# A four-layer graph network on one core: edge preparation moved into two earlier phases, and norm and dense product made one phase

## The chip, the core and the metric

One NeuronCore of a Trainium2 chip runs the whole program. Its engines work side by side and meet by semaphores: TensorE (PE in the rows; PEld is its loading of stationary operands), VectorE (DVE), ScalarE (ACT), GpSimd (POOL) and SyncE (SP), and 16 DMA engines that move data. The metric is the device time of one execution in microseconds. The kernel before took 6511.56 us, the median of three runs (6511.35 to 6515.23).

## What is computed

The graph has N = 3125 nodes with D = 128 features and E = 100000 edges, sorted by destination. Four layers follow each other, and each ends in `x = layernorm(x + layer(x))`:

```python
x = _layernorm(x + L0(x))   # two transformer convolutions, 8 heads
x = _layernorm(x + L1(x))   # [x, mean of x over the edges] @ W.T + b
x = _layernorm(x + L2(x))   # GINE: three message layers over the edges
x = _layernorm(x + L3(x))   # attention by source, one layer
# L2, one message layer:
m   = relu(h[src] + edge_attr @ W_ee + b_ee) * edge_weight
agg = segment_sum(m, dst)
h   = relu(mlp((1 + eps) * h + agg))
# _layernorm: (x - mean) / sqrt(var + 1e-5) over the 128 features
```

The change lies around L1 and L2. L1 is a dense product of x and a mean aggregation; L2 begins with the dense product h = x W_enc + b_enc and then needs, for each edge, its source row, its 16 attributes, its weight, and whether it has the same destination as its neighbour.

## The kernel before

Nodes are held as 25 tiles of 128 partitions x 128 features, side by side in one tile `x` (128 x 3200 floats); `skip` and `work` are of the same shape. `big` is one large scratch area cut into named parts. `QUADS` are the tiles in groups of four: six of four tiles and one of one.

The program is a row of phases, each an `nc.Block()`: every engine gets its own list of instructions, and at the block's end all engines meet. Semaphores got by `fresh` are cleared on POOL behind the block. `Chain` (`link(...)`) makes VectorE wait for the end of each instruction before it begins the next.

From the second convolution to the first message layer the phases are, in this order:

1. `node_math(conv_nodes)` (L1445 to L1457 with `norm_ops`, L988 to L1000): the sums of the heads are divided (L1450), the skip path and x are added (L1451, L1455), and the norm follows: reduce (L992), subtract (L994), square (L995), reduce (L996), square root on ScalarE (recorded as L1024), scale (L1000). Each is one VectorE instruction over 128 x 3200.
2. `node_linear` (L1031 to L1093): SP loads weights (L1042), PE transposes x (L1064), ScalarE copies the turned tiles (L1056), PE multiplies (L1079), VectorE adds the bias (L1092).
3. `by_src(x, False)` (L1468 to L1522), the mean aggregation: 30 indirect loads of 128 x 3200 counts from `snap_tab` by POOL (L1481) into a ring of nine buffers; VectorE takes the difference of two of them (L1505, 25 times), PE multiplies x with it into seven PSUM banks (L1520, 14 passes each). POOL's load v waits for PE's product v - 9.
4. `node_math(per_degree)` (L1560 to L1562): one over the degree.
5. `turn_back` (L1529 to L1551): the sums leave PSUM (L1536, L1548) and are multiplied back node by node (L1564, L1565).
6. `node_math(add_norm)` (L1567 to L1569): add x, then the norm as in 1.
7. `node_linear` again, for h = x W_enc + b_enc.
8. `gine_prep` (L1123 to L1217): VectorE clears the tiles (L1172 to L1177), then SP loads destinations, sources and weights of all edges (L1142), small weights (L1143 to L1146) and all attributes (L1148, 6.4 MB), and writes the table of h that the edges gather from (L1151). VectorE computes which neighbours share a destination (L1184 to L1217), with small products on PE between (L1159 to L1167). SP waits for all of it at the end (L1152 to L1154).
9. `gine_edges`, `gine_nodes`, three times. In `gine_edges` POOL gathers 8 rows per edge unit from `h_tab` (L1241, 784 per layer), PE multiplies attributes (L1281), VectorE joins, weights and scans, ScalarE writes the sums out.

After the third message layer, `node_math(add_norm)` and `node_linear` come once more, for L3, then `by_src(skip, True)` with attention.

Of the kernel before, what the change touches and what calls it, by code (L numbers as in the profile page):

```python
# [40 lines left out]
U = 5  # L41
# [39 lines left out]
def build(nc, a, out):  # L81
    ctx = ExitStack()
    with ctx:
# [904 lines left out]
        def norm_ops(link, act_sqrt, src3, dst3):  # L988

            mean, var, inv, tmp = (col25[:, k * NT:(k + 1) * NT] for k in range(4))  # L990
            bc = lambda c: c.unsqueeze(2).to_broadcast([P, NT, D])
            link(nc.vector.tensor_reduce(mean, src3, AX_X, ALU.add))  # L992
            link(nc.vector.tensor_scalar(mean, mean, 1.0 / D, None, ALU.mult))
            link(nc.vector.tensor_tensor(dst3, src3, bc(mean), ALU.subtract))  # L994
            link(nc.vector.tensor_tensor(sq3, dst3, dst3, ALU.mult))  # L995
            link(nc.vector.tensor_reduce(var, sq3, AX_X, ALU.add))  # L996
            link(nc.vector.tensor_scalar(var, var, 1.0 / D, LN_EPS, ALU.mult, ALU.add))
            act_sqrt(var, tmp)
            link(nc.vector.reciprocal(inv, tmp))
            link(nc.vector.tensor_tensor(dst3, dst3, bc(inv), ALU.mult))  # L1000

# [25 lines left out]
        SQRT = (ACT.Sqrt, col25[:, NT:2 * NT], col25[:, 3 * NT:4 * NT], {})  # L1027

        QUADS = [(t, min(t + 4, NT)) for t in range(0, NT, 4)]

        def node_linear(source, loads, cols, parts, tabs):  # L1031

            with ExitStack() as ph:
                w_in, tr_done, copied, mm_done, evac, tab_out = fresh(ph, "w_in", "tr_done", "copied", "mm_done", "evac", "tab_out")
                turned = [stages[:, k * 512:(k + 1) * 512] for k in range(2)]
                wide = cols > D
                evacs_of = (lambda t: t * len(parts)) if wide else (lambda t: -(-t // 4))
                with nc.Block() as block:
                    @block.sync
                    def _(sp):  # L1040
# [3 lines left out]
                        for lo, hi in QUADS if tabs else ():  # L1044
                            sp.wait_ge(evac, evacs_of(hi))
# [13 lines left out]
                    def _(pe):  # L1059
# [9 lines left out]
                        for g, (lo, hi) in enumerate(QUADS):  # L1069
# [3 lines left out]
                            if not wide:  # L1073
                                later(pe, evac, g - 5)
                            for t in range(lo, hi):
                                if wide:
                                    later(pe, evac, evacs_of(t - 5))
                                to = bank[2 + t % 6][:, 0:cols] if wide else bank[2 + g % 6][:, (t - lo) * D:(t - lo + 1) * D]
                                nc.tensor.matmul(to, turned[g % 2][:, (t - lo) * P:(t - lo + 1) * P], wgt[:, 0:cols], start=True, stop=True).then_inc(mm_done, 1)  # L1079

                    @block.vector
                    def _(dve):
                        dve.wait_ge(w_in, 16 * len(loads))
                        for g, (lo, hi) in enumerate(QUADS):
                            if wide:
# [37 lines left out]
        def gine_prep():  # L1123

            with ExitStack() as ph:
# [6 lines left out]
                with nc.Block() as block:  # L1132
# [5 lines left out]
                    def _(sp):  # L1138
                        sp.wait_ge(cleared, 6)
                        for tile, flat in ((dst_nat, a["dst"]), (src_nat, a["src"]), (weight_nat, a["edge_weight"])):  # L1140
                            for to, of in natural_parts(tile, flat, 1):
                                sp.dma_start(to, of).then_inc(idx_in, 16)  # L1142
# [548 lines left out]
```

## Time and profile before

| | us |
|---|---|
| median of 3 runs | 6511.56 |
| the profiled execution | 6520.61 |
| its span, first to last instruction | 6518.6 |
| VectorE busy in the span | 4148.0 (64%) |
| GpSimd busy in the span | 4155.0 (64%) |
| TensorE busy in the span | 3342.7 (51%) |
| mean granted TensorE clock | 0.673 |

The profile names each instruction by engine, line and the tiles that it writes and reads. "idle before" is the time its engine stood still ahead of it, with what it waited for; `<-issue` is time without a wait that the profile shows, `PEq` and `DVEq` are sequencers at a phase's meeting point. The granted clock is a share of TensorE's 2.4 GHz: 0.50 is its lower level of 1.2 GHz. "SPq" rows are the issue of a DMA, not its transfer.

### The profile page before, as it was taken

What the parts mean: (1) busy time and instruction counts of PE and PEld (TensorE: products, weight loads), DVE (VectorE), ACT (ScalarE), POOL (GpSimd) and SP (SyncE); (2) the same over time, 40 slices, a digit from 0 to 9 for tenths busy, and PEclk for the clock granted to TensorE, in tenths of its full rate; (3) what the DMA queues carried; (4) which work ended last, traced back from release to release, by engine and by line L of the source; (5) the groups of instructions that cost most, each with busy time, mean ns of one, the idle gap of its engine ahead of it and who ended that gap; (6) DMA issues with size and microseconds to landing.
All of it is one profiled execution on the core that took longest, in us unless ns stands there. A gap on an engine that the chain in (4) does not pass through costs nothing. (4 is left out here: it accounts for less than half of the span.)

```text
span 6518.6 us, 51793 instructions
## 1 busy us (share of the span) xinstructions
PE 3342.7 (51%) x13823; PEld 2045.6 (31%) x13823; DVE 4148.0 (64%) x5215; ACT 1487.1 (23%) x3019; POOL 4155.0 (64%) x4233
## 2 busy tenths in 40 slices
PE   3577777746777776553333333433334333433363
PEld 2355555635556555331111111111111111111131
DVE  5577777776777777564555554555554555555597
ACT  0122222201222221002322232222322223222121
POOL 0477777736777775216777776777776777777220
PEclk7677777776776777776556666555556666665686
DMA  0566666627666664543333332333332333333341
GB/s 22 156 198 198 197 195 194 193 82 205 192 194 197 195 198 132 200 148 101 104 107 104 104 104 86 107 104 104 107 105 89 101 104 106 106 104 102 123 158 60
DMA packets 540777, 877.86 MB, mean 135 GB/s; under 512 B 85157, under 2 KB 383121, under 8 KB 532318
## 3 DMA queue, kind: packets, MB, share of 16 engines
q0 software_dynamic: 167776, 479.21, 25.6%
q1 hardware_dynamic: 372728, 395.35, 18.8%
q8 instruction: 130, 2.13, 0.1%
q14 instruction: 143, 1.17, 0.1%
HBM read 553.75 MB, written 320.47 MB: 134 GB/s over the span
## 5 line engine op out<-in xcount | busy, mean ns | idle before, releaser
L1241 POOL DMA_INDIRECT big<-h_tab,big x2352 | 2224.4, 946 | 801.7 <-issue 801.7
L1281 PE MATMUL psum<-big 128*128 128x512 f32 x1176 | 1085.0, 1077 | 1787.4 <-ACT big L1264 1787.2
L633 POOL DMA_INDIRECT big<-kv_tab,big x1664 | 1649.5, 991 | 534.8 <-issue 499.6
L1307 DVE TENSOR_TENSOR psum<-psum,big 128x1024 f32<-128x1024 f32 x294 | 555.5, 1890 | 1363.5 <-DMA big<-h_tab,big 1363.5
L1281 PEld LDWEIGHTS psum<-big 128*128 128x128 f32 x1176 | 342.7, 322 | 2364.4 <-ACT big L1264 2060.9
L1258 ACT COPY big<-big 128x1024 f32<-128x1024 f32 x294 | 563.3, 1916 | 2103.5 <-DVE big L1301 2103.5
L762 PE MATMUL psum<-big 128*128 128x136 f32 x3328 | 715.2, 368 | 480.0 <-DVE big L820 302.2
L762 PEld LDWEIGHTS psum<-big 128*128 128x128 f32 x3328 | 613.9, 259 | 576.1 <-issue 548.4
L672 ACT COPY big<-psum 125x128 f32<-125x128 f32 x1408 | 376.5, 267 | 1488.8 <-PE psum L718 1409.4
L1301 DVE TENSOR_TENSOR_SCAN big<-big,psum 128x1024 f32<-128x1024 bf16 x294 | 669.0, 2276 | 0.1
L710 PE MATMUL psum<-big 128*128 x4992 | 585.6, 265 | 104.5 <-DVE big L791 104.2
L718 PE MATMUL psum<-big 128*128 128x128 bf16 x1408 | 567.5, 403 | 113.5 <-ACT big L672 60.0
L807 DVE TENSOR_TENSOR big<-psum,big 128x512 f32<-128x512 f32 x416 | 286.5, 689 | 418.3 <-DMA big<-kv_tab,big 376.9
L710 PEld LDWEIGHTS psum<-big 128*128 128x128 bf16 x4992 | 447.4, 117 | 194.9 <-issue 111.3
L1481 POOL DMA_INDIRECT big<-snap_tab,small x60 | 138.5, 2309 | 408.3 <-PE psum L1520 266.2
L1313 DVE SCALAR_TENSOR_TENSOR psum<-psum,big 128x1024 f32<-128x1024 f32 x294 | 359.4, 1223 | 0.4
L843 DVE SCALAR_TENSOR_TENSOR big<-big,psum 128x136 f32<-128x136 f32 x832 | 292.2, 351 | 50.8 <-PE psum L762 6.1
L1266 ACT CAST big<-big 128x1024 bf16<-128x1024 f32 x294 | 304.2, 1035 | 0.0
L820 DVE TENSOR_TENSOR big<-big,small 128x512 f32<-128x512 f32 x416 | 286.4, 688 | 0.0
L812 DVE TENSOR_TENSOR big<-big 128x512 f32<-128x512 f32 x416 | 284.9, 685 | 0.2
L817 DVE TENSOR_REDUCE big<-big 128x32 f32<-128x512 f32 x416 | 282.1, 678 | 0.7
L718 PEld LDWEIGHTS psum<-big 128*128 128x128 bf16 x1408 | 209.8, 149 | 219.9 <-issue 171.5
(385 smaller groups left out, 3242.6 us busy)
## 6 DMA issues: line engine op xcount, KB each, us to landing
run_tab<-big SPq DMA_DIRECT2D x294, 512.0 KB, 2.7
snap_tab<-big SPq DMA_DIRECT2D x176, 448.0 KB
item_tab<-big SPq DMA_DIRECT2D x208, 272.0 KB, 4.2
big<-loc_tab SPq DMA_DIRECT2D x104, 512.0 KB, 4.7
big<-h_tab,big POOLq DMA_INDIRECT x2352, 2.5
big<-kv_tab,big POOLq DMA_INDIRECT x1664
snap_tab<-big SPq DMA_DIRECT2D x176, 52.0 KB
kv_tab<-big SPq DMA_DIRECT2D x12, 512.0 KB, 2.6
```

The costliest lines, as they stand in the source:

```text
L633: nc.gpsimd.indirect_dma_start(out=kv[:, b % SLOTS, k, :], out_offset=None, in_=kv_tab, in_offset=bass.IndirectOffsetOnAxis(ap=src_item[:, ...
L672: nc.scalar.copy(snaps[0:125, n % 16 * P:(n % 16 + 1) * P], bank[7][0:125, 0:P]).then_inc(snapped, 1)
L710: ins_ = nc.tensor.matmul(bank[b % 2][:, k * P:(k + 1) * P], hot_T[b // 4 % 2][:, (b % 4 * 4 + k) * P:(b % 4 * 4 + k + 1) * P], q3[:, j * ...
L718: nc.tensor.matmul(bank[7][:, 0:P], key_hot[n // 8 % 2][:, n % 8::8], lo_hot[n // 8 % 2][:, n % 8::8], start=first_c + n == 0, stop=True, ...
L762: ins_ = nc.tensor.matmul(region(2 * b + i), hot[b % 2][:, k * P:(k + 1) * P], va[b % 2][:, k, :], start=s == 0, stop=s == 1)
L1241: nc.gpsimd.indirect_dma_start(out=got[j % RING][:, k * D:(k + 1) * D], out_offset=None, in_=h_tab, in_offset=bass.IndirectOffsetOnAxis(ap ...
L1258: nc.scalar.copy(rows_out[j % ROWS].rearrange("p (t f) -> p f t", f=D), sums_ft[j % DEEP].rearrange("p (f t) -> p f t", t=UNIT)).then_inc( ...
L1266: nc.scalar.copy(inner_x[j % DEEP].rearrange("p (f t) -> p f t", t=UNIT), inner[:, UNIT * j:UNIT * (j + 1)].unsqueeze(1).to_broadcast([P, ...
L1281: ins_ = nc.tensor.matmul(bank[2 * (j % DEEP) + k][:, :], ea_T[j % DEEP], w_blocks[:, k * 512:(k + 1) * 512], start=True, stop=True)
L1301: nc.vector.tensor_tensor_scan(sums_ft[j % DEEP], inner_x[j % DEEP], msg[j % DEEP], 0.0, ALU.mult, ALU.add).then_inc(run_done, 1)
L1307: nc.vector.tensor_tensor(by_feature(msg[j % DEEP]), by_feature(msg[j % DEEP]), got[j % RING].rearrange("p (t f) -> p f t", f=D), ALU.add) ...
L1313: nc.vector.scalar_tensor_tensor(by_feature(msg[j % DEEP]), by_feature(msg[j % DEEP]), 0.0, weight_nat[:, UNIT * j:UNIT * (j + 1)].unsquee ...
```

## The change

- `norm_ops` is gone. A new phase `norm_linear` does the join with x, the norm and the dense product in one block, quad by quad: VectorE joins and takes the mean, ScalarE squares (one instruction per tile, with the sum taken on the way) and takes the root, VectorE scales, PE transposes, ScalarE copies, PE multiplies, VectorE adds the bias. It takes the place of phases 1's norm and 2, of 6 and 7, and of the same pair ahead of L3. For L2 it also writes `h_tab`.
- `gine_prep` is gone. Its memsets, index, weight and small loads, and its chain on VectorE and PE are spread over `by_src(x, False)`, behind the steps n = 4, 8, 12, 14, 18 and 20; `per_degree` is the last of them.
- The edge attributes load in `turn_back`, issued by SP and not waited for there; POOL clears their last rows and makes the node numbers.
- What needs the edge counts (eight short instructions) stands at the head of the first `gine_edges`.
- Areas in `big` and the divisor `den` are placed anew; `gine_edges`, `gine_nodes` and the first convolution are otherwise the same.

```diff
+        def norm_linear(loads, joined, work3, scale_of=None, h_table=False):
...
+                    @block.scalar
+                    def _(act):
+                        for n in range(last + 1):
+                            if n < last:
+                                lo, hi = QUADS[n]
+                                act.wait_ge(centre, n + 1)
                                 for t in range(lo, hi):
+                                    nc.scalar.activation(x3[:, t, :], work3[:, t, :], ACT.Square, bias=mean[:, t:t + 1], accum_out=var[:, t:t + 1]).then_inc(squared, 1)
+                            if n > 0:
+                                lo, hi = QUADS[n - 1]
+                                act.wait_ge(varied, n)
+                                nc.scalar.activation(root[:, lo:hi], var[:, lo:hi], ACT.Sqrt).then_inc(rooted, 1)
+                                act.wait_ge(tr_done, n)
+                                later(act, mm_done, n - 2)
+                                nc.scalar.copy(turned[(n - 1) % 2][:, 0:(hi - lo) * D], bank[(n - 1) % 2][:, 0:(hi - lo) * D]).then_inc(copied, 1)
+                    @block.tensor
+                    def _(pe):
+                        for g, (lo, hi) in enumerate(QUADS):
+                            pe.wait_ge(normed, hi)
+                            later(pe, copied, g - 1)
...
+                            if g == 0:
+                                pe.wait_ge(w_in, 16 * len(loads))
+                            pe.wait_ge(copied, g + 1)
...
+                        def centred(g):
+                            lo, hi = QUADS[g]
+                            joined(link, lo, hi, work3)
+                            link(nc.vector.tensor_reduce(mean[:, lo:hi], work3[:, lo:hi, :], AX_X, ALU.add))
+                            nc.vector.tensor_scalar(mean[:, lo:hi], mean[:, lo:hi], -1.0 / D, None, ALU.mult).then_inc(centre, 1)
...
+                        def scaled(g):
+                            lo, hi = QUADS[g]
+                            dve.wait_ge(rooted, g + 1)
+                            link(nc.vector.reciprocal(inv[:, lo:hi], root[:, lo:hi]))
+                            for t in range(lo, hi):
+                                nc.vector.tensor_scalar(x3[:, t, :], work3[:, t, :], mean[:, t:t + 1], inv[:, t:t + 1], ALU.add, ALU.mult).then_inc(normed, 1)
...
+                        for n in range(last + 3):
+                            if n < last:
+                                centred(n)
+                            if 0 < n <= last:
+                                spread_of(n - 1)
+                            if n >= 3:
+                                product_out(n - 3)
+                            if 0 < n <= last:
+                                scaled(n - 1)
...
+                    @block.sync
+                    def _(sp):
+                        if not attention:
+                            sp.wait_ge(cleared, 5)
+                            for tile, flat_ in ((dst_nat, a["dst"]), (src_nat, a["src"]), (weight_nat, a["edge_weight"])):
+                                for to, of in natural_parts(tile, flat_, 1):
+                                    sp.dma_start(to, of).then_inc(idx_in, 16)
...
+                        between = {} if attention else {4: compared, 8: linked, 12: runs, 14: spread_out, 18: rows_back, 20: degrees}
...
+                            if n in between:
+                                between[n]()
...
+                            if n == 12:
+                                pe.wait_ge(to_pe, 3)
...
+        def turn_back(per_tile, after, attributes=False):
...
+                        if attributes:
+                            (to0, of0), (to1, of1), (to2, of2) = natural_parts(ea_nat, a["edge_attr"].rearrange("e c -> (e c)"), EA)
+                            sp.dma_start(to0[0:96], of0[0:96]).then_inc(ea_in, 16)
+                            sp.wait_ge(cleared, 1)
+                            sp.dma_start(to0[96:112], of0[96:112]).then_inc(ea_in, 16)
+                            sp.dma_start(to1, of1).then_inc(ea_in, 16)
+                            sp.dma_start(to2, of2).then_inc(ea_in, 16)
...
+                        if layer == 0:
+                            pe.wait_ge(totalled, 1)
+                            nc.tensor.matmul(bank[5][:, 0:1], upper[:, :], in_all[:, 0:1], start=True, stop=True).then_inc(in_all_done, 1)
+                            pe.wait_ge(ea_in, 16 * 4)
                         turn(0)
...
-        gine_prep()
+        norm_linear([(wgt[:, 0:D], a["L2_W_enc"]), (bias[:, 0:D], a["L2_b_enc"].to_broadcast([P, D])),
+                                (bn[:, :], a["L2_bn"]), (epsb[:, 0:3], a["L2_eps"].to_broadcast([P, 3]))], plus_x,
+                    area(6400, NT * D).rearrange("p (t d) -> p t d", d=D), h_table=True)
```

## Rows read from the trace of the kernel before

**Rows 1.** Stages: length, busy us of PE, PEld, DVE, ACT, POOL, clock, DMA share, GB/s.
```profile
2623.90:2669.40 45.50, 10.56 (x75) 10.00 (x75) 34.59 (x20) 5.23 (x9) 0.00 (x0) 0.59 0.02 5
2669.40:2697.10 27.70, 0.00 (x0) 0.00 (x0) 0.00 (x1) 0.00 (x0) 8.47 (x9) 0.55 0.90 374
...
2760.00:2800.00 40.00, 40.00 (x105) 18.66 (x104) 25.63 (x17) 0.00 (x0) 16.70 (x8) 1.00 0.81 304
...
2838.30:2854.80 16.50, 12.18 (x50) 11.99 (x50) 9.39 (x30) 1.73 (x4) 0.00 (x0) 0.90 0.00 0
2855.10:2877.50 22.40, 0.00 (x0) 0.00 (x0) 21.61 (x9) 0.22 (x1) 0.00 (x0) 0.54 0.00 0
2877.50:2893.60 16.10, 11.60 (x75) 11.04 (x75) 4.35 (x7) 3.79 (x7) 0.00 (x0) 0.69 0.05 10
2893.60:2911.50 17.90, 0.00 (x0) 0.00 (x0) 7.96 (x6) 0.00 (x0) 2.91 (x1) 0.61 0.27 74
2911.50:2931.90 20.40, 3.04 (x12) 2.78 (x12) 17.46 (x32) 0.00 (x0) 0.00 (x0) 0.50 1.02 249
2931.90:2949.00 17.10, 0.00 (x0) 0.00 (x0) 0.00 (x0) 0.00 (x0) 0.00 (x0) 0.50 0.77 174
...
6081.60:6103.90 22.30, 0.00 (x0) 0.00 (x0) 21.61 (x9) 0.22 (x1) 0.00 (x0) 0.52 0.00 0
6103.90:6122.50 18.60, 11.75 (x75) 11.19 (x75) 4.35 (x7) 3.79 (x7) 0.00 (x0) 0.66 0.10 22
```
**Rows 2.** The longest waits from 2690 to 2840 us: waiter, releaser, total, times, longest.
```profile
DVE big L1505 <- DMA big<-snap_tab,small: 73.5, 25, 27.8
...
PE psum L1520 <- DVE big L1505: 32.0, 1, 32.0
```
**Rows 3.** Timeline: start, length, engine, line, count, idle before; the aggregation.
```profile
2700.71 4.64 PE L1520 MATMUL psum<-big,x 128*128 128x512 f32 x5 [32.01 <-DVE big L1505]
...
2819.53 18.65 PE L1520 MATMUL psum<-big,x 128*128 128x512 f32 x49
...
2826.87 3.49 DVE L1505 SCALAR_TENSOR_TENSOR big<-big 128x3200 f32<-128x3200 f32 x1 [2.47 <-DMA big<-snap_tab,small]
```
**Rows 4.** Timeline of the preparation's loads and of the gathers behind it.
```profile
2911.56 1.09 SPq L1148 DMA_DIRECT2D big<-in_edge_attr  x3
...
2950.50 0.98 POOL L1241 DMA_INDIRECT big<-h_tab,big  x1 [53.31 <-issue]
```
**Rows 5.** What SP's queue waited for, 2600 to 3000 us.
```profile
SPq L1154 <- DMA big<-in_edge_attr: 28.1, 1, 28.1
```
**Rows 6.** DMA issues, 2902 to 2955 us: count, KB each, median us to landing.
```profile
h_tab<-big SPq DMA_DIRECT2D x5, 320.0 KB, 30.6
```
**Rows 7.** Groups of instructions by form: busy us, mean ns, idle before.
```profile
L1056 ACT COPY big<-psum 128x512 f32<-128x512 f32 x30 | 17.6, 587 | 163.9 <-PE psum L1064 163.9
...
L1024 ACT ACT_TABLE_LOAD x4 | 5.1, 1283 | 45.1 <-PEq L872 38.5 <-PEq L1531 6.5
...
L1403 ACT ACTIVATE skip<-skip 128x128 f32<-128x128 f32 x3 | 0.9, 296 | 0.0
```
**Rows 8.** Timeline: VectorE's form with a scalar per partition, four in a row.
```profile
2616.41 0.87 DVE L931 TENSOR_SCALAR big<-big 128x128 f32<-128x128 f32 x4
```
**Rows 9.** Groups by line, whole span: the 512-column VectorE form, and the gathers.
```profile
L1241 POOL DMA_INDIRECT big<-h_tab,big x2352 | 2224.4, 946 | 801.7 <-issue 801.7
...
L812 DVE TENSOR_TENSOR big<-big 128x512 f32<-128x512 f32 x416 | 284.9, 685 | 0.2
```
**Rows 10.** Timeline from a last table row of h to the next gather.
```profile
3990.18 0.29 DVE L1386 SCALAR_TENSOR_TENSOR big<-skip,bias 128x128 f32<-128x128 f32 x1
...
3994.68 0.95 POOL L1241 DMA_INDIRECT big<-h_tab,big  x1 [15.88 <-issue]
```
**Rows 11.** Timeline: transposes at either clock, and the first product's wait.
```profile
6111.04 1.12 PE L1064 MATMUL psum<-ident,x 128*128 128x128 f32 x4 [5.64 <-DMA big<-in_L_ln_b]
...
6117.65 0.60 PE L1064 MATMUL psum<-ident,x 128*128 128x128 f32 x4
```

More of the change, by code:

```diff
@@ L1072, in _ @@
                             pe.wait_ge(copied, g + 1)
-                            if not wide:
-                                later(pe, evac, g - 5)
                             for t in range(lo, hi):
[L1076 to L1079, printed above, removed]
+                                later(pe, evac, len(parts) * (t - 5))
+                                nc.tensor.matmul(bank[2 + t % 6][:, 0:cols], turned[g % 2][:, (t - lo) * P:(t - lo + 1) * P], wgt[:, 0:cols], start=True, stop=True).then_inc(mm_done, 1)
                     @block.vector
@@ L1106, in build @@
+        RUN = 16
+        run = area(10000, RUN * D)
+        ea_nat = area(10000 + RUN * D + NT * P + 176, J * EA)
+        ea_in, = dma_sems("ea_in")
+        assert 10000 + RUN * D + NT * P + 176 + J * EA <= o and J % RUN == 0
         h_plus = area(3200, NT * D)
@@ L1109, in build @@
         b_edge = bias[:, 3 * D:4 * D]
-        takes = area(29512, NT * P)
+        takes = area(10000 + RUN * D, NT * P)
+        colB = small[:, 700:708]
         ROWS_NAT = P * J
@@ L1277, in _ @@
                         for j in range(UNITS):
+                            if layer == 0 and j == 2:
+                                pe.wait_ge(counts_read, 1)
                             pe.wait_ge(copied, j + 1)
@@ L1484, in _, with clear @@
                     @block.vector
                     def _(dve):
+                        link = Chain(dve, step)
+                        def clear():
+                            nc.vector.memset(dst_nat, PHANTOM).then_inc(cleared, 1)
+                            nc.vector.memset(src_nat, ZROW).then_inc(cleared, 1)
+                            nc.vector.memset(weight_nat, 0.0).then_inc(cleared, 1)
+                            nc.vector.memset(w_loaded, 0.0).then_inc(cleared, 1)
+                            nc.vector.memset(zero, 0.0).then_inc(cleared, 1)
@@ L1524, in build @@
+                            if n == 12:
+                                pe.wait_ge(to_pe, 3)
+                                for k in range(2):
+                                    ins_ = nc.tensor.matmul(bank[7][:, (k + 1) * P:(k + 2) * P], srows[:, k * P:(k + 1) * P], ident[:, :], start=True, stop=True)
+                                ins_.then_inc(from_pe, 1)
         agg_T = area(0, NPF)
         BANKS = -(-NP // 512)
-        def turn_back(per_tile, after):
+        def turn_back(per_tile, after, attributes=False):
```

319 lines of the change are left out of this document (160 added, 159 removed).

## The prediction

> **What bounds the kernel now.** The page's own chain of waits reaches back only 1% of the span, so I read stages. The time of most of the program is set by GpSimd's gathers: 2352 in the message layers, 946 ns each and 0.3 us apart [rows 9]. The change leaves them alone, so all that it can win or lose lies between the second convolution's sums and the first gather, and in the norm and product ahead of L3. The busy time by stage [rows 1] shows there a row of short phases in which one engine works and the others stand. From 2623.9 to 2669.4 us VectorE is busy for 34.6 of 45.5 us with the norm's full-width passes. From 2669.4 to 2697.1 only DMA works, at 374 GB/s. Then TensorE is busy for 40.0 of 40 us at full clock: the aggregation is bound by the product, and in its waits [rows 2] TensorE waits once, 32.0 us before the first product, and never again. Then come 16.5 us of turning back, 22.4 of norm, 16.1 of product, 17.9 and 20.4 of preparation, and 17.1 us in which no engine works and DMA is at 0.77. What ends these is in SP's waits: 28.1 us for the edge attributes [rows 5], and the first gather starts at 2950.5 [rows 4]. The old stretch from the norm's start at 2855.1 to that gather is 95.4 us; the stretch ahead of L3 from 6081.6 to 6122.4 is 40.8.
>
> **Norm and product as one phase.** I build the loop of one quad. VectorE: a 512-column pass is 0.69 us [rows 9], 0.72 with the chain's gap (estimate). Behind the second convolution the join has three and the reduce is the fourth, with the small mean scale 3.1 us; in the other two phases the join has one, 1.65 us. ScalarE then squares four tiles. The row before shows no square and no sum taken on the way; the nearest is 0.296 us for a 128-column activation [rows 7], so I take 0.35 each, 1.4 us, with bounds of 1.2 (no extra) and 2.1 (0.5 each plus waits). The root is 0.22, the one ScalarE instruction of the old norm [rows 1]. VectorE waits for it, takes a reciprocal of four columns (0.2) and scales four tiles in 0.87 [rows 8]. These follow each other, with 0.3 for signals: 6.1 us a quad in the first phase, 4.6 in the others. Beside that chain lie PE's transposes (1.12 at the lower clock, 0.60 at full clock [rows 11]), ScalarE's copy (0.59 [rows 7]) and the bias (0.69): they fit under the next quad's join, with nothing to spare in the short loop. VectorE's other share of the old norm, subtract and square at 3.5 us each, goes to the scaling and to ScalarE.
>
> After the second convolution: 1.75 for the divisors, 3.1 + 3.1 to fill, 2.9 to the first scaled quad, four more quads at 6.1, then the last, short quad and the drain of transpose, copy, product and bias, 7.4: 42.7 against 45.5. Thirteen semaphores are cleared behind it instead of six, 0.5 us. I take a gain of 2.4, bounds -3 and +5. Ahead of L3: 3.3 + 2.9 + 4 x 4.6 + 6.4 = 31.0 against 40.8. Its weights took until 6111.04, 7 us into the old product phase [rows 11]; now they are asked for at the phase's start and wanted 8 us in, so they are in time. I take 9.5, bounds 6 and 11.
>
> **The aggregation.** The moved loads of 2893.6 to 2911.5 are 74 GB/s x 17.9 us = 1.3 MB [rows 1]. SP asks for them some 4.5 us into the phase, behind five memsets on VectorE, which stands idle there for 27.8 us. They share the DMA engines with the counts on which the first difference waits, so that start moves by 1.3 MB at 374 to 420 GB/s: 3.1 us lost (bounds 0 and 5). TensorE's own part of the preparation was 3.04 us at the lower clock [rows 1], less one product that goes elsewhere; it is now inside the engine that bounds the phase: 2.0 us lost (bounds 1.3 and 3). VectorE's moved chain is 17.46 less 3.8 for the table of h, 1.9 for the node comparison and 1.1 for the edge counts: 10.7 us. What hides it: VectorE's idle 73.5 less the first 27.8 is 45.7 us over 24 steps [rows 2], 1.9 each; and its last difference ends at 2830.3 while TensorE, which needs 5.4 us a step (14 of the 0.38 us passes in [rows 3]), still has 49 passes from 2819.5 to 2838.2, so its last step began at 2832.8, a lead of 2.4. The longest piece, behind n = 12, is 4.3 us: idle and lead cover it. If they did not, only its excess of a microsecond or two would be lost. The waits for PE sit four steps behind what they ask for and are met. The two degree instructions lose their own phase: 1.0 us won. In sum 4.1 us lost.
>
> By the Trainium skill, page "SBUF — State Buffer", section "Who interferes with whom", VectorE's copies and tensor_scalars in a two-port mode lock out GpSimd for their whole length; the moved copies would hold up POOL's loads of counts by at most their own few microseconds. Nothing in these rows shows such a block.
>
> **From the turning back to the first gather.** The attributes are now asked for when the sums turn back. POOL's memset (5632 columns, 5 us at the rate of the 2.91 us that 3200 columns of node numbers took [rows 1]) and the numbers end 8 us in, under the 15 us of that phase. The load itself took from 2911.56 [rows 4] to 2945.0 (2916.9, SP's last issue, plus 28.1 [rows 5]), 33.4 us. So it ends about 18 us after the norm begins, and with it comes **a new wait**: the norm phase's weights are on SP's queue behind it. That a queue keeps them back is seen in the table writes of h, which stood behind the attributes and took 30.6 us to land [rows 6], where 320 KB would be done in one or two. TensorE wants the weights at 7.9 us (first quad scaled at 6.2, transposed and copied), gets them at 18.5 (bounds 14 and 20), and nothing behind the first quad can be turned until then, since the wait stands ahead of the second quad's transposes; ScalarE waits behind these, and VectorE behind ScalarE. Two quads of work are done by then: from 18.5, product 1.9, transpose and copy 1.8, square and root 1.7, scaling 1.2: the third quad is scaled at 25.1; three more at 4.6 with the short one end at 36.9; drain 4.1: 41.0. The second addition for the table lies in VectorE's waits. From the last table row to the next gather was 4.2 us between layers [rows 10]. So the stretch is 45.2 instead of 95.4: 50.2 us won. The eight instructions at the head of the first message layer, 3.5 us, lie under its first eight gathers (10 us), and the attributes are long there. Four more semaphores per message layer and three for `by_src`: 1.0 us lost.
>
> **Sum.** 2.4 - 4.1 + 50.2 + 9.5 - 1.0 = 57.0 us. The profiled execution was 6520.6, its span 6518.6, so its span would be 6461.6. The median of the runs lies 9.0 under that execution; taken from it, 6511.6 - 57.0 = 6454.6. Adding the bounds that can fall together, 50 to 65 is plain for the stated mechanism: 6446 to 6463.
>
> **Rivals.**
> *The weights overtake* (0.12). If the attributes don't hold up the small loads, the middle stretch is 31.3 + 4.2 = 35.5 and 10 us more are won: 6445. Against it stands the 30.6 us row.
> *ScalarE's steps are longer* (0.12). If a square with its sum costs 0.6 us and the signals 0.3 more, the loop grows by 1.3 us in 17 quads: 22 us back, 6476. No row of a square speaks against it.
> *Squares and roots need different tables* (0.05). A table load is 1.28 us [rows 7]. Two per quad are 14 a phase, 18 us, 54 in three phases: 3 us are left, 6508. For it: no row shows a square beside a root. Against it: copies and relus run between the roots with no load. The Trainium skill, page "ScalarE: Activation LUTs", section "Table sets: the hidden batching unit", says that functions should be batched by set since a switch costs a load, and that cheap ones (relu, copy, identity, abs) are in every set; the square is not in its list.
> *The aggregation slows TensorE* (0.03), the slower side. Passes took 0.93 us at the aggregation's start and 0.38 at its end, at full clock [rows 3]. If TensorE must wait on VectorE behind n = 12 and falls to its lower level, each step costs 7.6 us more; 14 passes of 0.55 us; from 8 such steps on the whole gain is gone, and with the 13 left it is 99 - 57 = 42 slower: 6554. For it: the clock was at half after idle stretches [rows 1]. Against it: a lead of 2 us and the full clock in all of the middle.
> *The overlap does less than it says* (0.04): the attributes come far later than 18 us, or the counts are starved through the whole phase: 6485.
>
> **How the numbers follow.** The stated mechanism has 0.64 at 6454.6. With the overtaking weights and part of the longer steps the range is 6440 to 6476. Faster by over 0.2% (13 us, which is about what a measurement of this kernel tells from none) holds in all cases but the tables and the slow clock: 0.92, 0.05 same, 0.03 slower.
>
> **What would show it.** Right: TensorE's one wait in the first norm phase with a table is for its weights, about 10 us; no table load between a square and a root; quads 4.6 us apart ahead of L3; first count difference 3 us later; TensorE still without idle time in the aggregation. Wrong: that wait missing, or quads 6 us apart, or an idle TensorE behind n = 12.

## The result and the profile after

The changed kernel takes 6475.1 us (median of 5 runs, 6473.2 to 6481.1) against 6511.6 (5 runs, 6508.3 to 6517.6): a ratio of 0.9946, 95% interval 0.9935 to 0.9956. A second comparison of the same pair gave 0.9947 (0.9933 to 0.9960). So the change wins 36 us where 57 were forecast, and the time lies at the upper end of the range, outside it by the ratio (0.9946 x 6511.56 = 6476.4). The sign was right, the size was not.

All that follows is read by stages: from one landmark instruction to the next. The forecast's stages, before and after (us):

| from, to | before | after | forecast |
|---|---|---|---|
| second convolution's sums, first load of counts | 46.88 | 48.03 | 44.5 |
| to the first difference of counts | 26.40 | 33.65 | 29.5 |
| to the last product of the aggregation | 141.02 | 141.01 | 143.0 |
| to turning back | 1.34 | 0.30 | 0.3 |
| turning back | 15.62 | 15.62 | 15.6 |
| norm's start, first gather | 95.36 | 53.97 | 45.2 |
| three message layers | 3067.99 | 3066.75 | +1.0 for semaphores |
| norm and product ahead of L3 | 41.13 | 35.05 | 31.6 |

The stages of the change itself give 1.15 + 7.25 - 0.01 - 1.04 - 41.39 - 6.08 = -40.1 us. In a second pair of profiles they give -0.27 + 7.61 + 0.74 - 1.04 - 41.88 - 5.46 = -40.3. The runs gave 36.5 and 35.3, with intervals that take in 40, though a third comparison, below, came out lower still.

The busy time by stage, to be laid beside [rows 1] (the columns are the same: length, busy us of PE, PEld, DVE, ACT and POOL, clock, DMA share, GB/s):

```profile
2619.50:2665.70 46.20, 19.90 (x75) 15.59 (x75) 32.92 (x83) 16.14 (x65) 0.00 (x0) 0.50 0.02 5
2665.70:2701.20 35.50, 0.00 (x0) 0.00 (x0) 3.19 (x6) 0.00 (x0) 8.43 (x9) 0.50 0.92 331
2760.00:2800.00 40.00, 40.00 (x109) 18.96 (x109) 30.65 (x27) 0.00 (x0) 14.74 (x8) 1.00 0.79 292
2842.30:2857.90 15.60, 12.19 (x50) 11.99 (x50) 8.90 (x28) 1.73 (x4) 7.70 (x2) 0.89 0.96 206
2857.90:2882.70 24.80, 1.12 (x4) 0.72 (x4) 8.80 (x25) 5.51 (x27) 0.00 (x0) 0.51 0.89 135
2882.70:2912.00 29.30, 18.77 (x75) 14.82 (x75) 19.50 (x51) 8.99 (x39) 0.00 (x0) 0.56 0.15 56
6042.30:6077.30 35.00, 19.91 (x75) 15.59 (x75) 22.35 (x67) 14.21 (x64) 0.00 (x0) 0.51 0.07 12
```

Four things stand out. The norm and product of the second convolution are one phase, and its 46.2 us are no less than the 45.5 of the two: TensorE is busy for 19.90 us with the same 75 instructions that took 10.56 in [rows 1], since its clock is at 0.50. The counts load at 331 GB/s instead of 374. In the aggregation TensorE is busy for all of the 40 us, with four small instructions more. And of the 24.8 us from 2857.9 to 2882.7 TensorE works for 1.12: it waits.

For what it waits, the timeline tells (start, length, engine, line, operation, and in brackets the idle time before it and its releaser), with the first gather behind it, which answers to [rows 4]:

```profile
2842.47 0.32 SPq L1640 DMA_DIRECT2D big<-in_edge_attr  x1
...
2848.76 0.25 SPq L1644 DMA_DIRECT2D big<-in_edge_attr  x1
...
2858.06 0.35 SPq L1080 DMA_DIRECT2D wgt<-in_L_W_enc  x1
...
2864.46 1.12 PE L1110 MATMUL psum<-ident,x 128*128 128x128 f32 x4 [7.81 <-DVE x L1140]
...
2882.70 2.08 PE L1117 MATMUL psum<-wgt,big 128*128 128x128 f32 x8 [17.13 <-DMA epsb<-in_L_eps]
...
2885.67 0.59 ACT L1102 COPY big<-psum 128x512 f32<-128x512 f32 x1 [17.84 <-PE psum L1110]
...
2912.08 1.29 POOL L1219 DMA_INDIRECT big<-h_tab,big  x1 [61.19 <-issue]
```

The weights are asked for at 2858.1, behind the attributes, and the first product that needs them starts at 2882.7, 24.6 us behind the phase's first VectorE instruction (2858.11). The DMA issues from 2840 to 2915 us say it from the queue's side (count, KB, median us from issue to landing; the last row is the one of [rows 6] again, without attributes ahead of it):

```profile
wgt<-in_L_W_enc SPq DMA_DIRECT2D x1, 64.0 KB, 22.9
bias<-in_L_b_enc SPq DMA_DIRECT2D x1, 64.0 KB, 22.8
...
h_tab<-big SPq DMA_DIRECT2D x6, 256.0 KB, 2.0
```

The longest waits from 2690 to 2845 us answer to [rows 2]: VectorE waits less, since the moved preparation fills its gaps, and TensorE again waits once.

```profile
DVE big L1585 <- DMA big<-snap_tab,small: 67.6, 20, 31.4
...
PE psum L1602 <- DVE big L1585: 39.4, 1, 39.4
```

### The profile page after: what moved, and what is told of

It is laid out like the page before. It is cut to its first block and busy times, and to the rows that moved or that the text cites. A ratio compares the mean times of both kernels' runs of the same rounds, so it can differ in the third digit from the quotient of the medians.

```text
span 6473.4 us, 52111 instructions
## 1 busy us (share of the span) xinstructions
PE 3347.9 (52%) x13821; PEld 2034.4 (31%) x13823; DVE 4132.0 (64%) x5381; ACT 1517.7 (23%) x3187; POOL 4139.2 (64%) x4234
## 3 DMA queue, kind: packets, MB, share of 16 engines
q0 software_dynamic: 167776, 479.21, 25.7%
## 5 line engine op out<-in xcount | busy, mean ns | idle before, releaser
L1265 PEld LDWEIGHTS psum<-big 128*128 128x128 f32 x1176 | 342.7, 322 | 2358.6 <-ACT big L1242 2055.1
L762 PE MATMUL psum<-big 128*128 128x136 f32 x3328 | 691.6, 358 | 502.7 <-DVE big L820 316.2
L762 PEld LDWEIGHTS psum<-big 128*128 128x128 f32 x3328 | 592.5, 250 | 598.4 <-issue 569.7
```

Source lines behind the costliest of these rows:

```text
L762: ins_ = nc.tensor.matmul(region(2 * b + i), hot[b % 2][:, k * P:(k + 1) * P], va[b % 2][:, k, :], start=s == 0, stop=s == 1)
L1265: ins_ = nc.tensor.matmul(bank[2 * (j % DEEP) + k][:, :], ea_T[j % DEEP], w_blocks[:, k * 512:(k + 1) * 512], start=True, stop=True)
```

## The experiments

All of them but the last pair ran on other chips of the same kind, where the kernel before takes 7636 to 7648 us: there the convolutions and message layers are longer for both kernels. The stages of the change are not: the changed kernel itself has 48.03, 33.54, 141.29, 0.30, 15.62, 54.57 and 35.05 there. So experiments are read by these stages, and by ratio only against a kernel on the same chip. The first five, and the one with unneeded products, were timed once each, so their stages are all the evidence there is. The theory at this point: each of four misses has a cause of its own (the attributes' load is slow and holds back the weights; loads of index lists slow down the loads of counts; a table load lies on the path; the loop of quads is slowed by a TensorE at its lower clock). The rival to the first is that something else in the new phase is late; to all, that what is won ahead of the gathers is given back in them.

**Weights ahead of the attributes.**
```diff
+        for dst, src in L2_LOADS:
+            sp.dma_start(dst, src).then_inc(w_early, 16)
         sp.dma_start(to0[0:96], of0[0:96]).then_inc(ea_in, 16)
...
```


> The four small loads of the L2 norm phase (weights, bias, bn, eps) are issued at the head of the turning back, ahead of the edge attributes; all else as in the changed kernel. In the changed kernel TensorE waited 17.1 us for them and the stretch from the norm's start to the first gather was 54.0 us. If the wait is the price of their place behind the attributes, TensorE's wait is gone, its first product starts 8 to 9 us into the phase instead of 24.6, and the stretch is 38 to 41 us (the pipeline had done two quads in the wait, so 13 to 16 come back). Rival: the attributes' own transfer disturbs the phase however the queue is ordered (table rows of h then stand behind the attributes, and SP waits for them at the end): the stretch stays above 48 us.

Measured: norm's start to first gather 38.77 us instead of 53.97, and 7591.0 us. TensorE's wait is gone from the timeline, and nothing else takes its place:
```profile
3509.40 0.69 DVE L1168 TENSOR_TENSOR big<-skip,x 128x512 f32<-128x512 f32 x1 [0.52 <-PEq L1629]
...
3517.64 2.04 PE L1119 MATMUL psum<-wgt,big 128*128 128x128 f32 x8 [0.77 <-ACT big L1104]
...
3548.17 1.29 POOL L1221 DMA_INDIRECT big<-h_tab,big  x1 [45.99 <-issue]
```
The first product is now 8.2 us into the phase, where the forecast wanted its weights (7.9). So the late weights cost 15.2 us of this stretch.

**The attributes in short packets**, four loads of 12544 bytes a row for each of 50176:
```diff
-        sp.dma_start(to0[0:96], of0[0:96]).then_inc(ea_in, 16)
+        for k in range(4):
+            sp.dma_start(to0[0:96, k * C:(k + 1) * C], of0[0:96, k * C:(k + 1) * C]).then_inc(ea_in, 16)
...
```


> The attributes load in pieces of 784 columns x 4 per row, so that a DMA packet is 12544 bytes instead of 50176; order and queue as in the changed kernel. In the trace a packet of 50176 bytes took 3.6 us, which is 14 GB/s on one DMA engine, and one of 12800 bytes of the counts 0.48 us, 27 GB/s. If length is what makes them slow, the load ends 16 to 18 us after its first issue instead of 38, TensorE's wait for its weights falls from 17.1 to under 3 us, and the stretch from norm to gather from 54.0 to 38 to 42 us. If the rate is set by where the rows lie (source pitch or partitions) and not by their length, packets of 12544 bytes take 0.9 us, and stretch and wait stay as they are.

Measured: TensorE waits 15.0 us instead of 17.1, the stretch is 51.9 instead of 54.0. A packet of 12544 bytes to the partitions 0 to 95 takes 0.85 us, 14.7 GB/s in each of the 16 engines or 236 in all; to the partitions 96 to 126 it takes 1.83 (told apart by their order). The length of a packet is not what makes the load slow.

**The attributes on ScalarE's queue**, the weights on SP's:
```diff
-        sp.dma_start(to0[0:96], of0[0:96]).then_inc(ea_in, 16)
+        act.dma_start(to0[0:96], of0[0:96]).then_inc(ea_in, 16)
...
```


> The attributes are issued from ScalarE's queue instead of SP's, 3 us later in the same phase; everything else as in the changed kernel. If the weights waited because one queue keeps its order, they now land within 5 us of their issue and TensorE's wait (17.1) falls under 3 us; the stretch from norm to gather is then 38 to 42 us. If the DMA engines alternate packet by packet between queues, each 512-byte row of a weight waits behind one 50176-byte packet of 3.6 us; with 8 such rows per engine and load the weights come 20 us or more late, and the wait stays near 17 us.

Measured: wait 17.4 us, stretch 53.4: no change.
```profile
3546.20 2.07 PE L1117 MATMUL psum<-wgt,big 128*128 128x128 f32 x8 [17.45 <-DMA epsb<-in_L_eps]
...
3574.65 1.29 POOL L1219 DMA_INDIRECT big<-h_tab,big  x1 [60.58 <-issue]
```
A queue of their own doesn't save the weights. In the packet records their 256 rows of 512 bytes begin to move 22.7 us after the turning back began instead of 30.3, but 180 of them start only at 35 to 40, as the attributes' last packets (of 50176 bytes, 4.4 us each) leave the engines. What holds them back is the engines' work, not the order on one queue. The Trainium skill, page "DMA: Bandwidth & Descriptors", section "Queues, rings and completion order", says that each engine takes turns between queues packet by packet. That agrees with these starts only in part. From 22 to 32 us 76 small rows move, two or three at each change of a long packet. But they were asked for from 15.6 us on, and from 17 to 22 us 17 long packets end without a small row behind them; why is not shown.

**The attributes over all 128 partitions.** Of each row's 12544 words the first 6912, as far as the last, short row reaches, go out in two loads over all partitions; the rest keeps the old split.
```diff
-        sp.dma_start(to0[0:96], of0[0:96]).then_inc(ea_in, 16)
+        for lo, hi in ((0, T // 2), (T // 2, T)):
+            sp.dma_start(ea_nat[:, lo:hi], bass.AP(flat.tensor, flat.offset + lo, [[J * EA, P], [1, hi - lo]])).then_inc(ea_in, 16)
+        sp.dma_start(to0[0:96, T:], of0[0:96, T:]).then_inc(ea_in, 16)
...
```


> The edge attributes' first 6912 columns go out as two loads over all 128 partitions (8 rows to each of the 16 DMA engines) instead of 96, 16 and 15 partitions; the remaining columns keep the old three loads. Weights stay behind them on the queue. Theory (rate set by how many partitions, and so ports, a load reaches): the last attribute bytes land some 10 us sooner, TensorE's wait for the weights falls from 17.1 us to below 7, and the stretch from the norm's start to the first gather from 54.0 to 41-46 us. Rival (the rate is the packets' or the queue's, whatever partitions they reach; 230 GB/s stays): wait 15 to 17 us, stretch 52 to 54. All other stages as in the changed kernel.

Measured: wait 4.4 us, stretch 41.3.
```profile
3528.15 2.08 PE L1117 MATMUL psum<-wgt,big 128*128 128x128 f32 x8 [4.43 <-DMA epsb<-in_L_eps]
...
3557.55 1.29 POOL L1219 DMA_INDIRECT big<-h_tab,big  x1 [48.51 <-issue]
```
The packet records of both kernels, in us from the start of the turning back:
```
kernel          bytes   packets  first    last end   mean us   GB/s of one engine
changed         50176   127       0.92    38.21      4.42      11.4
all partitions  13824   256       0.95    10.27      0.56      24.9
all partitions  22528   127       9.71    25.81      1.82      12.4
```
The same bytes from the same place, on the same queue, move at twice the rate where a load goes to 128 partitions, and back at the old rate where it goes to 96, 16 and 15. Since the short packets above, of nearly this length, ran at 14.7, it isn't their length. That the partitions share ports is not in a trace; the Trainium skill, page "SBUF — State Buffer", section "Door 1: The DMA port swizzle", says that the rate depends on how many of 16 ports the partitions reach. By its table 96 to 111 and 112 to 126 reach four each, which agrees with the slow tail. But by the same table 0 to 95 reach all 16, so the number of ports does not explain the 14.7 there; that cause stays open.

**The index loads behind the first difference.**
```diff
                             sp.wait_ge(cleared, 5)
+                            sp.wait_ge(diff, 1)
```


> SP's loads of indices and small weights in the aggregation begin only behind the first difference. In the changed kernel the first difference came 33.7 us after the first load of counts, 26.4 before the change; I had expected 3.1 us for 1.3 MB. If the two queues' packets alternate and so slow the counts, the first difference is back at 26 to 27 us, and since TensorE then has a lead of 2 to 5 us, the rest of the aggregation keeps its 141 us: 7 us won. Rival: the same packets then hold up later counts, TensorE runs out of its lead and waits 3 to 7 us in the middle: nothing won.

Measured: first difference after 26.24 us instead of 33.65 (before: 26.40), the aggregation behind it 143.00 instead of 141.01. Over the stretch ahead of the first difference, in the columns of [rows 1]:
```profile
3333.70:3359.90 26.20, 0.00 (x0) 0.00 (x0) 1.95 (x4) 0.00 (x0) 8.42 (x9) 0.50 0.95 392
```
That is 392 GB/s; between the same two landmarks the kernel before had 393 and the changed kernel 348. Packet by packet, from 4.5 to 21 us into the stretch: before, and here, counts move at 428 GB/s in packets of 12800 bytes (0.48 us each). In the changed kernel they share the engines with 381 packets of 3136 bytes, take 0.58 us, and move at 299, while both together reach 356. The loss is thus 7.4 us for 1.2 MB of index lists, more than the 3.1 us of their bytes: the sum of both is slower than counts alone. Whether that comes from the short packets or from the 112 and 15 partitions that these loads go to was not tried. 5.4 us of the loss stay won. Of the 2.0 lost again, 1.57 are a second wait of TensorE in the middle of the aggregation, for a difference (at 3438.2 us), which the changed kernel does not have: so the rival, that a lead gained at the start is used up later, is right for that part.

**The old two phases on the first two norms.** The code of the kernel before, with a short phase for the table of h behind the second; all else as changed.
```diff
-        norm_linear([...], plus_x, area(6400, NT * D)..., h_table=True)
+        node_math(add_norm, [SQRT])
+        node_linear_old(x, [...], D, [skip], [])
...
```


> Norm and product ahead of the aggregation and ahead of the first message layer go back to the two old phases (the table of h gets a short phase of its own behind them); the norm ahead of L3 and all that was moved stay changed. Theory (the join of the two phases gives back on the first of these what it costs there): the stretch from the second convolution's sums to the first load of counts is 46.9 us again instead of 48.0, and in the message layer the weights' wait disappears in the norm, so that the stretch from the norm's start to the first gather is 22.4 + 16.1 + some 6 for the table phase + 4.2 = 49 us (45 to 52), that is 5 us less than the 54.0 of the joined phase although it is the slower code: joining the phases brought nothing there. Rival (the joined phase is worth what I forecast in the message layer too): stretch over 56 us. L3's stage 35.05 in both.

Measured: 0.9947 (0.9933 to 0.9961). Norm's start to first gather: 46.1 us, against 54.0 of the joined phase and 38.8 of the joined phase with early weights. As the kernel was changed, joining there loses 8 us; with the weights in time it wins 7. The second convolution's stage is 48.00, not the 46.9 expected: here TensorE came up to its full clock a quad later than in the kernel before, its second group of products taking 1.80 us instead of 1.06. So in that place one phase or two come to the same.

**Unneeded products to keep TensorE's clock up.**
```diff
+                            for _k in range(14 if g == 0 else 6):
+                                nc.tensor.matmul(bank[g % 2][:, 0:P], ident[:, :], ident[:, :], start=True, stop=True)
                             pe.wait_ge(normed, hi)
```


> TensorE does 14 unneeded 128x128 products before the first and 6 before each other quad of the three joined norm phases, into the bank that the transposes then overwrite. Theory (the quads ahead of L3 are 4.8 us apart partly because TensorE runs at the low clock: 1.12 instead of 0.60 for four transposes, about 2.07 instead of 1.16 for four products): the transposes show 0.6, quads are about 4.3 us apart and L3's stage falls from 35.05 to 30-33 us; the stage of the second convolution's norm falls by 1 to 2 from 48.0. Rival (the loop is bound by ScalarE and VectorE, TensorE's part lies beside it): quads stay 4.8 apart, L3's stage 34 to 35.5; if the extra products only delay the transposes, above 36.

Measured: L3's stage 34.06, above the expected 30 to 33; the second convolution's stage 1.0 longer where 1 to 2 less was expected, and the stretch to the first gather 1.0 longer too. First the changed kernel's transposes and reciprocals, one group for each quad, then the experiment's:
```profile
6053.45 1.12 PE L1110 MATMUL psum<-ident,x 128*128 128x128 f32 x4 [0.86 <-DVE x L1140]
...
6056.86 0.18 DVE L1138 RECIPROCAL big<-big 128x4 f32<-128x4 f32 x1 [1.28 <-ACT big L1099]
...
6061.66 0.18 DVE L1138 RECIPROCAL big<-big 128x4 f32<-128x4 f32 x1 [1.28 <-ACT big L1099]
```
```profile
7192.45 0.66 PE L1112 MATMUL psum<-ident,x 128*128 128x128 f32 x4 [0.78 <-DVE x L1142]
...
7195.73 0.18 DVE L1140 RECIPROCAL big<-big 128x4 f32<-128x4 f32 x1 [1.15 <-ACT big L1099]
...
7198.62 0.40 ACT L1095 ACTIVATE x<-big 128x128 f32<-128x128 f32 x1 [0.23 <-DVE big L1130]
...
7200.40 0.18 DVE L1140 RECIPROCAL big<-big 128x4 f32<-128x4 f32 x1 [1.15 <-ACT big L1099]
```
The clock did rise (1.12 to 0.66 for four transposes, the granted clock from 0.51 to 0.91), and the quads are 4.67 us apart instead of 4.79. Expected were 4.3: that part of the theory is wrong. The squares now wait 0.23 us for VectorE's mean instead of for the copy; the loop is VectorE's join, reduce and mean (1.6), four squares (1.5), root and reciprocal (0.4), scaling (1.0) and the signals between them, in a row. The clock matters in the drain, where each step waits for TensorE, and there extra products ahead of the short last quad stand in its way. Left out there, they give 32.73 (the last experiment).

**Three mends together.** Early weights, late index loads, and one root of no use at the head of the second convolution's phase:
```diff
+                        if scale_of is not None:
+                            nc.scalar.activation(small[:, 1100:1101], ident[:, 0:1], ACT.Sqrt)
...
```


> The changed kernel with three mends: the weights of the first message layer's norm are asked for ahead of the attributes; the loads of the layers' index lists wait for the first difference of counts; one root of no use at the head of the second convolution's norm phase takes ScalarE's table load out of the path. Theory (the three losses are separate and add up): norm's start to first gather 38.8 us (-15.2), counts load to first difference 26.3 (-7.4), aggregation behind it +1 to +2, second convolution's stage 46.7 (-1.3): 22 us under the changed kernel, so 0.991 of before on a chip like the first one's. Rival (what is won ahead of the first gather is given back in the gathers behind it, or the loads of index lists come too late for their use behind n = 12): the three stages as said, but VectorE or TensorE waits in the aggregation for over 5 us more, or the first message layer is longer by some us than in the other runs on the same chip; gain 10 us or less.

Measured: 0.9927 (0.9902 to 0.9951), and by stages 46.60, 26.14, 141.37 and 38.77, as expected within 0.2, but for the aggregation, which is 0.4 longer instead of 1 to 2 (TensorE again waits a second time, for 0.44 us). The table load, in the changed kernel
```profile
2629.08 1.28 ACT L1099 ACT_TABLE_LOAD   x1
2630.38 0.21 ACT L1099 ACTIVATE big<-big 128x4 f32<-128x4 f32 x1
```
lies now 0.04 us ahead of the phase's first VectorE instruction, and the first reciprocal comes 9.69 us into it instead of 11.11: 1.4 us, the load and little more.

**The changed kernel on the chip of the mends.**

> The changed kernel itself, on the same chip as the version with four mends, so that both have the same kernel before beside them. By stages as in its first profile: 48.0 from the second convolution's sums to the first load of counts, 33.7 to the first difference, 141 to the last product, 54.0 from the norm to the first gather, 35.05 ahead of L3. If the gain is only these stages it is 36 to 42 us less than before whatever the chip: a ratio of 0.9946 where before takes 6510, 0.995 where it takes 7640. If the change also moved the gathers, the ratio would be farther from that than its interval.

Measured: 0.9960 (0.9947 to 0.9973), 25.7 us. The stages are as expected, the ratio is only at the edge of its interval where 40 us should put it (0.9948).

**Four mends**, the three and the extra products ahead of L3's full quads but the last step:
```diff
+                            if scale_of is None and not h_table and g + 1 < last:
+                                for _k in range(14 if g == 0 else 6):
+                                    nc.tensor.matmul(bank[g % 2][:, 0:P], ident[:, :], ident[:, :], start=True, stop=True)
...
```


> The three mends (weights ahead of the attributes, index loads behind the first difference, table load off the path) and, ahead of L3 alone, 14 and 6 unneeded products of TensorE before each full quad. Theory: stages of 46.6, 26.2, 141.4 to 143, 38.8 and 34.0; together 23 us less than the changed kernel on this chip, 0.3% of it. Rival (a gain ahead of the gathers is given back in them, since the DMA engines and GpSimd set their pace): difference to the changed kernel under 10 us, with the stages as said and longer message layers.

Measured: 0.9926 (0.9914 to 0.9938), 7586.3 us against the changed kernel's 7612.3 on the same chip. The intervals of the two ratios don't overlap. The stages are 46.72, 26.14, 142.39, 39.00 and 32.73, 25.5 us under those of the changed kernel beside it; the runs gave 26.0. What is won ahead of the gathers is not given back in them. By stages this is the best version, 0.9 us under the three mends; the runs can't tell the two apart (0.9926 and 0.9927). The attributes over all partitions are not in it, and on the first chip it wasn't run.

**Both kernels again**, on a chip where the kernel before takes 6516 us, to see whether a part of the 40 us is given back elsewhere.

> The kernel before itself, profiled on the same chip as a second run of the changed kernel. Theory (what lies between the stages of the change is untouched, so the change is worth the 40 us of its stages on any chip): stages of 46.9, 26.4, 141, 1.3, 15.6, 95.4 and 41.1 as in its first profile; the ratio to itself is 1.000 within 0.0015; and the three message layers and the convolutions ahead of them differ from those of the changed kernel by no more than two profiles of the same kernel do (some 10 us each).

> The changed kernel again, beside the kernel before. Theory (40 us, the sum of its stages, on this chip too): a ratio of 0.9948, and together with the run before it about 0.995. Rival (a third of the gain is given back elsewhere where the chip is slower, since there 26 us were measured): a ratio of 0.9965, and message layers that are longer by some 5 us each in the changed kernel than in the kernel before.

Measured: the kernel before against itself 1.0003 (0.9994 to 1.0012); the changed one 0.9947 (0.9933 to 0.9960), 35.3 us. The message layers and what lies between them and L3 take 3133.1 us in the one and 3131.1 in the other: nothing is given back. The convolutions ahead of the change end at 2622.4 us in the one profile and at 2613.9 in the other, though both run the same code there, and the two profiled executions are 6520.5 and 6469.4 us: single profiles differ by more than what separates 36 from 40, so that difference stays open. It may be none, though all three comparisons (36.5, 25.7 and 35.3 us) lie under 40. In this second profile of the changed kernel the second convolution's stage is 46.71 instead of 48.03, since TensorE's clock came up in the drain.

## Why the prediction was right and wrong

**The new wait, right in place, mis-sized and misread in kind.** The forecast had TensorE wait for its weights behind the attributes, ScalarE and VectorE behind it. That is what happens. But the weights come at 24.6 us, not at 18.5 (bounds 14 and 20). The failed step is the attributes' load taken as the 33.4 us of the kernel before, ended when its last bytes land, and the weights at once behind it: the load now took 38.2 us, in 96, 16, 15 and 1 rows instead of 112, 15 and 1. By the packet records the first 96 rows are there after 25 us (before: 22) and the last 31 take 13 more (10). Split off as a load of their own, 16 rows take 6.3 us each, where the last 16 packets of the old load of 112 took 3.6; the split is thus a likely part of the loss, though no run undid it. The weights came another 1.6 us behind its end. And the row of [rows 6] was read as a queue's order. For the weights it was one of busy engines: another queue changed nothing. The last rival, attributes that come far later and counts that are slowed, names in part what happened, but priced it at 6485.

**The steps of the quads, right; their number, wrong.** After the second convolution the quads are 6.12 us apart (forecast 6.1), ahead of L3 4.79 (4.6); the first scaled quad of L3 is there at 6.3 (6.2). But there are six full quads and a short one, and the forecast has a step for five full ones and the short one, in each of the three phases. From the fifth scaled quad to the end it gave 7.4 us in the first phase and 6.4 in the last; by the trace it is 9.3 in both, to the last bias. In the middle phase it gave 15.9 from the third scaled quad to the last table row, and it is 19.2. That is 1.9, 2.9 and 3.3 us of the miss. Behind the fifth quad the reciprocals come 3.64 and 3.25 us apart, less than 4.79, since no full join is left. In L3 the extra products, left out ahead of the short quad, took 2.3 us out of the stage, 1.8 of them behind the fifth scaled quad: so 1.8 of that phase's 2.9 is the price of the lower clock, at which four products take 2.07 us instead of the 1.16 of that experiment.

**The squares** take 0.40 us and 0.19 for reading the sum, one every 0.38: 1.54 a quad for 1.4. The rival of longer steps is refuted as a mechanism, and that the time it gave (6476) is about the one measured is chance.
```profile
2624.45 0.40 ACT L1095 ACTIVATE x<-big 128x128 f32<-128x128 f32 x1 [42.85 <-DVE big L1128]
2624.75 0.19 ACT L1095 ACTIVATION_READ_ACCUMULATOR x<-big 128x1 f32 x1
2624.85 0.39 ACT L1095 ACTIVATE x<-big 128x128 f32<-128x128 f32 x1
```

**The tables.** Squares and roots follow each other with no load between them, so that rival is gone. The one load there is was on no term of the sum: in the kernel before it stood ahead of a ScalarE that was idle for 25 us, and here it lies between the first squares and their root. That is 1.4 us in the second convolution's stage. By the Trainium skill, page "ScalarE: Activation LUTs", section "What ACT_TABLE_LOAD costs", a switch would be about 2.66 us with a drain; the row is 1.28 and taking it off the path gave 1.4, so here the measurement decides.

**The counts' start.** Forecast 3.1 us, bounds 0 and 5, measured 7.3. The failed step is the charge by bytes: 1.2 MB at full rate. With the index loads beside the counts, the sum of both moved at 356 GB/s instead of 428.

**TensorE's small products** cost 2.0 in the forecast at the lower clock's 3.04 us. At the full clock, between passes, they cost 0.23, 0.45 and 0.45 us in the three steps that hold them, 1.1 in sum. That it shows as nothing is chance: the first step of 14 passes took 7.1 us instead of 8.3, the clock having come up sooner, as this row shows beside the first of [rows 3] (15 instructions in 7.72 us, where before the first five took 4.64).
```profile
2704.74 7.72 PE L1602 MATMUL psum<-big,x 128*128 128x512 f32 x15 [39.38 <-DVE big L1585]
```
That TensorE never waits for the moved VectorE work was right, and so the slower side's rival is refuted for this kernel. The lead is small, though: with the index loads delayed TensorE did wait once, 1.57 us, and won 5.4 us all the same. The degree instructions' 1.0 us was right.

**The sum by its terms** (forecast less measured): second convolution 3.5, counts' start 4.2, small products -2.0, norm to gather 8.8, L3 3.4, semaphores -1.0, since the message layers are no longer: 16.9 of the 57.0 - 40.1. The second convolution's term is the table load (1.4), the end of the phase (1.9) and 0.2 in the steps between, while the 0.5 us for more semaphores came as forecast (1.84 us from the last bias to the first load of counts, before 1.34); in the second profile, where the clock rose in the drain, the term is 2.1. The term from norm to gather is the weights (6.1) and the sixth quad with its drain (3.3), less 0.6 from the last table row to the gather (3.65 us for 4.2). L3's 3.4 is its end (2.9) and its steps (0.8), less 0.3, since 9.5 was taken where the sum gave 9.8. The range failed because its bounds were those of single steps, and all the errors that weighed went the same way. Its own edge was slightly off as well: a gain of 50 us would be 6461.6, not 6463.

## What to carry to other kernels

Before a large load is moved ahead of a phase, ask which small loads that phase needs: put them ahead of it, since a second queue doesn't help while long packets fill the engines. Give a large load all 128 partitions, and start a secondary load when the one that gates has landed. Where a loop is costed, write down every iteration with its size, the odd last one too, and cost the drain at the clock TensorE has in that loop; what stood harmless in an idle stretch (a table load) has to be looked for again once the stretch is filled.

## What the runs showed of the hardware

The rate of a load depended on its partitions: 24.9 GB/s an engine over 128 (packets of 13824 bytes), 14.7 over 96 (12544 bytes), half of that over 16 and 15. Loads in packets of 3136 bytes beside those of 12800 brought the sum of both from 428 down to 356 GB/s. The moment at which TensorE's clock rises in the same code differs between executions and moves a stage of 47 us by 1.3. Six unneeded 128x128 products a quad held the granted clock at 0.91 instead of 0.51 and bought 0.12 us a quad in the loop; left out ahead of the short quad they bought 1.8 us in its drain.
